# Delta-rule scan of a vision tower: the read-out products stored in four blocks of four k values

## The chip, the cores and the metric

The kernel runs on one core of one Trainium2 chip, as one launch. The metric is device time in microseconds (us): the median of 3 runs. Engines are named as in the profile: PE is TensorE (PEld its weight loads), DVE is VectorE, ACT is ScalarE, POOL is GpSimd, SP is SyncE.

## The reference, cut to what matters

The program is a tower of four pairs of layers (attention and feed-forward of four kinds each) over 32 images of 64 tokens with 256 features. The change is in the attention of the second pair, a gated delta rule: per image and head (32 x 16 = 512 states) a 16 x 16 matrix S is carried through the 64 tokens.

```
def step(S, inp):
    qt, kt, vt, at, bt = inp
    Sd = at[..., None, None] * S
    u = vt - jnp.einsum('bhk,bhkv->bhv', kt, Sd)
    Sn = Sd + bt[..., None, None] * kt[..., None] * u[:, :, None, :]
    o = jnp.einsum('bhk,bhkv->bhv', qt, Sn)
    return (Sn, o)
```

`o`, the read-out, is the sum over k of q[k] * S[k, v]. It is not needed by the next step; it is normed, projected and added to the stream after the scan.

## The kernel before

The 512 states lie on 128 partitions in 4 groups (`CG = 4`), so that a partition holds 4 x 16 x 16 = 1024 fp32 numbers of state, ordered g, v, k. Two copies of the state, `S[0]` and `S[1]`, stand in PSUM (`banks`, two banks each) and take turns. Groups 0 and 1 are half 0, groups 2 and 3 are half 1. Each engine has its instructions in an order written out by hand, with semaphores between them. One turn t of the 64 does this:

- DVE, `read_queries(t - 3)` (line 1820): state times q, 1024 elements, from PSUM into `products` in SBUF. It waits until the buffer is free (`o_summed_pair`).
- DVE, `read_keys(t)` (line 1811): state times k for each half, 512 elements, into `prod`. It waits for PE's `state0` and `state1` of turn t - 2.
- DVE, the reduce of line 1845: u of turn t out of `prod`.
- POOL: a correction for the next turn (line 1906), then the outer product of k and u (line 1911), 1024 elements.
- ACT, `fade` (line 1607): four copies of a state group from one S into the other, times the gate. It also places v (line 1599) and copies finished read-outs out of PSUM (line 1614).
- PE, `add_outer` (line 1464): for each half the outer product is added into the state in PSUM by a matmul of 512 columns against the identity. Then `sum_pair` (line 1473), one half of a read-out of two turns: 8 matmuls against the identity, one for each of 8 values of k, which add up the products over k in PSUM. Each reads 128 columns (2 turns x 64 pairs g, v). In 18 of the turns two or three matmuls of `sum_squares` follow (line 1482).

An fp32 matmul stands as two MATMUL records in the trace, each with its weight load. So a turn has 4 records of line 1464 and 16 of line 1473.

`products` reuses the memory of q, the tile `chain_q` in the rows. Its two ring places hold two turns (s) each. Before, an element's place is r, s, n, k with n = (g, v), so that the 128 columns that a matmul of one k reads stand 16 fp32 apart, 64 bytes.

Other instructions of the same layer read or write a 4-byte element at a distance, and their rows are used below. The last index of the operand's own layout gives the distance:

```
1755  dve.tensor_reduce(n2[:, g, :], o[:, g, :, :].rearrange("p d t -> p t d"), AX.X, ALU.add)   # 64 apart: 256 bytes
1789  dve.tensor_reduce(n2[:, g, 1:], dots.rearrange("p d t -> p t d"), AX.X, ALU.add)           # 63 apart: 252 bytes
1852  dve.tensor_reduce(n2[:, :, a:b], last_squares[n].rearrange("p g d t -> p g t d"), ...)     # 10 apart, then 2 apart: 40 and 8 bytes
1614  act.copy(o[:, :, :, 2 * n:2 * n + 2], ...)          # written in runs of 2 elements, 8 bytes
2244  act.copy(sel ...)                                   # written in runs of 4 elements, 16 bytes
1596  act.copy(qt[:, :, g, :].rearrange("p t d -> p d t"), q[:, g, :, :])   # written 64 apart: 256 bytes
```

Of the kernel before, what the change touches and what calls it, by code (L numbers as in the profile page):

```python
# [13 lines left out]
ALU = mybir.AluOpType  # L14
# [17 lines left out]
HD = D // HEADS  # L32
# [16 lines left out]
CG = 4  # L49
# [24 lines left out]
def bcast(ap, axis, n):  # L74

    ap = ap.unsqueeze(axis)
    shape = [int(s) for s in ap.shape]
    shape[axis] = n
    return ap.to_broadcast(shape)
# [1053 lines left out]
def vit_rest(nc, io, banks, H, ident, ident_bf, minus_half, const, const_in, scores_all, top, which, gate, xn_rows,  # L1133
# [4 lines left out]
    with ExitStack() as ctx:  # L1138
# [44 lines left out]
        with ExitStack() as work:  # L1183
# [3 lines left out]
            with ExitStack() as buffers:  # L1187
                experts = expert_layer(nc, buffers, work_sem, io, banks, ident, const, const_in, scores_all, top, which, gate,
                                       xn_rows, token_rows, lambda sp: [load(sp) for load in loads])
            delta = delta_layer(nc, work_sem, io, banks, H, ident, minus_half, token_rows, gate, chains, rates, front,  # L1190
                                delta_chain_buffers(nc, work), experts["all_sent"],
                                [sem(f"stored_o{g}") for g in range(CG)], first_load(0), first_load(1),
# [55 lines left out]
LASTS = ((CUTS[-1], TOK - TAIL), (TOK - TAIL, TOK))  # L1248
LAST = TOK - CUTS[-1]
ROW = HD + 2  # L1250
SUM_PARTS = ((0, 3), (3, 6), (6, 9), (9, 12), (12, 14), (14, HD))


# [27 lines left out]
def delta_layer(nc, sem, io, banks, H, ident, minus_half, token_rows, gate, chains, rates, front, chain, all_sent,  # L1281
# [15 lines left out]
    q, k, v, o = (chain[n] for n in "qkvo")  # L1297
    ka, kb, qt = (chain[n] for n in ("ka", "kb", "q_by_time"))
# [7 lines left out]
    flat = made_all[:, :, :].rearrange(states)  # L1306
    n_prod = 2 * CG * HD * ROW
    prod_ring = flat[:, 0:n_prod].rearrange("p (r g v x) -> p r g v x", r=2, g=CG, v=HD)
# [7 lines left out]
    dots = rows_flat[:, n_zero:n_zero + HD * (TOK - 1)].rearrange("p (d t) -> p d t", d=HD)  # L1316
    u_ring = rows_flat[:, n_zero:n_zero + 2 * CG * HD].rearrange("p (r g v) -> p r g v", r=2, g=CG)
    u = [u_ring[:, i, :, :] for i in range(2)]
    products = q[:, :, :, :].rearrange("p g d t -> p (g d t)").rearrange("p (r s n k) -> p r s n k", r=2, s=2, k=HD)
    link = rate[:, :, 0, :]  # L1320

    def state(b):
        return banks[:, b:b + 2, :].rearrange("p b (g v k) -> p (b g) v k", v=HD, k=HD)

    S = [state(0), state(2)]
# [5 lines left out]
    def o_n2(n):  # L1331
        return banks[:, 6, CG * CUTS[n]:CG * CUTS[n + 1]].rearrange("p (g t) -> p g t", g=CG)

    def chunk_squares(n):
        return squares[:, :, 0:CG * (CUTS[n + 1] - CUTS[n])]
# [82 lines left out]
    def tensor(pe):  # L1418
# [48 lines left out]
        def sum_pair(n, half):  # L1467
            if half == 0:
                pe.wait_ge(sem("q_made"), 2 * n + 2)
                if n > 1:  # L1470
                    pe.wait_ge(sem("o_made"), n - 1)
            for k in range(HD // 2 * half, HD // 2 * (half + 1)):
                ins = pe.matmul(o_sum[n % 2].rearrange("p (s n) -> p s n", s=2), ident[:, :],  # L1473
                                products[:, n % 2, :, :, k], start=(k == 0), stop=(k == HD - 1))
            if half:
                ins.then_inc(sem("o_summed_pair"), 1)

        def sum_squares(n, part):
            if part == 0:
                pe.wait_ge(sem("o_squared"), n + 1)  # L1480
            for d in range(*SUM_PARTS[part]):
                ins = pe.matmul(o_n2(n), ident[:, :], chunk_squares(n)[:, d, :]
                                .rearrange("p (g t) -> p g t", g=CG), start=(d == 0), stop=(d == HD - 1))
            if part == len(SUM_PARTS) - 1:
                ins.then_inc(sem("o_summed"), 1)
# [54 lines left out]
        for t in range(TOK):  # L1540
            for h in range(2):
                add_outer(t, h)
            if t >= 3:
                sum_pair((t - 3) // 2, (t - 3) % 2)
            for n in range(IN_STEPS):
                if 0 <= t - CUTS[n + 1] - 5 < len(SUM_PARTS):
                    sum_squares(n, t - CUTS[n + 1] - 5)
        sum_pair((TOK - TAIL) // 2 - 1, 1)

    def scalar(act):  # L1550
# [66 lines left out]
        def mean_out(n):  # L1617
            act.wait_ge(sem("o_summed"), n + 1)
            act.activation(n2[:, :, CUTS[n]:CUTS[n + 1]], o_n2(n), ACT.Identity, scale=1.0 / HD, bias=small[:, 0:1]
                           ).then_inc(sem("on_mean"), 1)  # L1620
# [6 lines left out]
        def square_out(n):  # L1627
            act.wait_ge(sem("o_made"), CUTS[n + 1] // 2)
            if n:
                act.wait_ge(sem("o_summed"), n)  # L1630
            act.square(chunk_squares(n).rearrange("p d (g t) -> p g d t", g=CG),
                       o[:, :, :, CUTS[n]:CUTS[n + 1]]).then_inc(sem("o_squared"), 1)
# [69 lines left out]
        for t in range(TOK):  # L1702
# [8 lines left out]
            for n in range(IN_STEPS):  # L1711
                if t == CUTS[n + 1] + 4:
                    square_out(n)
                if t == CUTS[n + 1] + 5 + len(SUM_PARTS):
                    mean_out(n)
# [11 lines left out]
    def vector(dve):  # L1727
# [86 lines left out]
        def read_queries(j):  # L1814
            n = j // 2
            for h in range(2):
                dve.wait_ge(sem(f"faded{h}"), j + 1)
            if n >= 2:
                dve.wait_ge(sem("o_summed_pair"), n - 1)
            dve.tensor_tensor(products[:, n % 2, j % 2, :, :].rearrange("p (g v) k -> p g v k", g=CG),  # L1820
                              S[j % 2], bcast(qt[:, j, :, :], 2, HD), ALU.mult
                              ).then_inc(sem("q_made"), 1)

        def read_last(j):
# [7 lines left out]
        for t in range(TOK):  # L1832
            if t == 3:
                dve.wait_ge(sem("q_turned"), CG)
            if t >= 3:
                read_queries(t - 3)
            read_keys(t)
            for h in range(2):
                dve.wait_ge(sem(f"prod_made{h}"), t + 1)
            dve.wait_ge(sem("values_placed"), t + 1)  # L1840
            if t:
                dve.wait_ge(sem("corrected"), t)
            if t >= 2:
                dve.wait_ge(sem("outer_made"), t - 1)
            dve.tensor_reduce(u[t % 2], prod[t % 2], AX.X, ALU.add).then_inc(sem("u_made"), 1)  # L1845
        read_queries(TOK - 3)
        dve.wait_ge(sem("u_made"), TOK)
        read_last(TOK - 2)
# [1125 lines left out]
```

## Time and profile before

| what | value |
|---|---|
| median of 3 runs | 1425.77 us (1425.03 to 1426.86) |
| the profiled execution: its time, its span | 1428.93 us, 1427.0 us |
| PE, DVE, ACT, POOL busy | 1269.4, 803.3, 512.3, 421.9 us |
| mean granted clock of TensorE | 0.952 |
| the scan | from 661 to 1010 us of the span |

The span is first to last instruction of the profiled execution; its own time is 1.9 us more, and 3.2 us over the median of the runs. A group of the trace is a source line with its engine, operation and tile; "idle before" is the time in which the engine stood still just ahead of it, with what ended the wait. Ends of matmuls are modelled, so that the distance of two starts is the safer measure on PE.

### The profile page before, as it was taken

What the parts mean: (1) busy time and instruction counts of PE and PEld (TensorE: products, weight loads), DVE (VectorE), ACT (ScalarE), POOL (GpSimd) and SP (SyncE); (2) the same over time, 40 slices, a digit from 0 to 9 for tenths busy, and PEclk for the clock granted to TensorE, in tenths of its full rate; (3) what the DMA queues carried; (4) which work ended last, traced back from release to release, by engine and by line L of the source; (5) the groups of instructions that cost most, each with busy time, mean ns of one, the idle gap of its engine ahead of it and who ended that gap; (6) DMA issues with size and microseconds to landing.
All of it is one profiled execution on the core that took longest, in us unless ns stands there. A gap on an engine that the chain in (4) does not pass through costs nothing. (4 is left out here: it accounts for less than half of the span.)

```text
span 1427.0 us, 25711 instructions
## 1 busy us (share of the span) xinstructions
PE 1269.4 (89%) x9667; PEld 1020.9 (72%) x9667; DVE 803.3 (56%) x1721; ACT 512.3 (36%) x1256; POOL 421.9 (30%) x573
## 2 busy tenths in 40 slices
PE   6999994898999999873999999999589999979975
PEld 4666674898999999630777877778467777766753
DVE  3666667111212211788777677676457777742587
ACT  2545451121121111543433333333124444435456
POOL 0111111232233332533444344343112212101465
PEclk9999997899999999995999999999899999999985
DMA  4111101898888883790000000000200004006721
GB/s 133 42 46 46 34 13 68 340 366 317 318 334 318 318 325 131 199 270 15 1 0 1 0 1 1 0 1 0 77 13 10 11 11 182 1 2 250 222 73 60
DMA packets 82714, 162.29 MB, mean 114 GB/s; under 512 B 42976, under 2 KB 61536, under 8 KB 76576
## 3 DMA queue, kind: packets, MB, share of 16 engines
q1 hardware_dynamic: 63776, 114.44, 23.5%
q0 software_dynamic: 10224, 44.05, 7.9%
q10 hardware_dynamic: 8592, 2.16, 0.7%
q8 instruction: 78, 1.28, 0.4%
q14 instruction: 44, 0.36, 0.1%
HBM read 134.28 MB, written 26.35 MB: 113 GB/s over the span
## 5 line engine op out<-in xcount | busy, mean ns | idle before, releaser
L1473 PEld LDWEIGHTS banks<-chain_q,ident 128*128 128x128 f32 x992 | 202.8, 204 | 39.3 <-issue 28.7
L1473 PE MATMUL banks<-chain_q,ident 128*128 128x128 f32 x992 | 226.2, 394 | 0.0
L936 PE MATMUL banks<-rowsT,w_up 128*128 128x128 f32 x1716 | 201.2, 278 | 0.2 <-DMA w_up<-in_up_w 0.2
L936 PEld LDWEIGHTS banks<-rowsT,w_up 128*128 128x128 f32 x1716 | 198.0, 195 | 0.5 <-DMA w_up<-in_up_w 0.4
L1464 PE MATMUL banks<-xT_d,ident 128*128 128x512 f32 x256 | 126.9, 618 | 31.4 <-POOL xT_d L1911 28.7
L1607 ACT ACTIVATE banks<-banks,rate 128x256 f32<-128x256 f32 x252 | 99.6, 446 | 136.8 <-DVE made L1811 132.7
L1911 POOL TENSOR_TENSOR xT_d<-kb,ys 128x1024 f32<-128x1024 f32 x64 | 123.3, 1927 | 3.7 <-DVE ys L1845 3.7
L1811 DVE TENSOR_TENSOR made<-banks,ka 128x512 f32<-128x512 f32 x128 | 86.0, 688 | 44.1 <-PE banks L1464 40.4
L950 PE MATMUL banks<-w_down,hT 128*128 128x256 f32 x468 | 107.5, 379 | 0.6 <-DVE res L1115 0.6
L1105 DVE TENSOR_TENSOR hT<-banks,silu 64x128 f32<-64x128 f32 x39 | 11.0, 283 | 168.0 <-ACT silu L993 168.0
L1820 DVE TENSOR_TENSOR chain_q<-banks,q_by_time 128x1024 f32<-128x1024 f32 x62 | 75.6, 1219 | 42.1 <-PE banks L1473 42.1
L1464 PEld LDWEIGHTS banks<-xT_d,ident 128*128 128x128 f32 x256 | 49.1, 200 | 70.0 <-issue 30.4
L950 PEld LDWEIGHTS banks<-w_down,hT 128*128 128x128 f32 x468 | 85.9, 190 | 11.0 <-issue 1.0
L1845 DVE TENSOR_REDUCE ys<-made 128x64 f32<-128x1152 f32 x64 | 86.6, 1353 | 5.7
L878 POOL DMA_DIRECT2D w_down<-in_down_w x39 | 22.2, 568 | 189.9 <-PE banks L950 181.7
L1906 POOL TENSOR_TENSOR made<-ys,rate 128x64 f32<-128x64 f32 x63 | 19.7, 313 | 198.0 <-DVE ys L1845 198.0
L2067 POOL TENSOR_TENSOR agg_b<-agg_b,minus_half 128x1 f32<-128x1 f32 x48 | 28.3, 590 | 158.8 <-DVE agg_b L2293 157.6
L983 ACT COPY rowsT<-banks 128x256 f32<-128x256 f32 x39 | 14.5, 373 | 147.0 <-PE banks L114 147.0
L1115 DVE COPY res<-banks 128x256 f32<-128x256 f32 x39 | 16.6, 425 | 75.2 <-PE banks L950 75.2
L468 PE MATMUL banks<-w_tok,patches 128*128 128x256 f32 x192 | 51.7, 408 | 7.1 <-DMA patches<-in_patches 7.1
L108 PE MATMUL banks<-ident 128*128 128x128 f32 x328 | 42.7, 286 | 12.1 <-PEq L92 12.1
L108 PEld LDWEIGHTS banks<-ident 128*128 128x128 f32 x328 | 40.9, 201 | 13.4 <-issue 13.0
(328 smaller groups left out, 2312.0 us busy)
## 6 DMA issues: line engine op xcount, KB each, us to landing
w_up<-in_up_w SPq DMA_DIRECT2D x39, 1408.0 KB, 6.1
w_down<-in_down_w POOLq DMA_DIRECT2D x39, 768.0 KB, 5.0
inter<-res_x SPq DMA_DIRECT2D x16, 512.0 KB, 4.0
back<-inter SPq DMA_DIRECT2D x15, 512.0 KB, 3.9
patches<-in_patches SPq DMA_DIRECT2D x16, 384.0 KB, 3.3
f<-in_f SPq DMA_DIRECT2D x6, 1024.0 KB, 11.8
ys<-token_rows SPq DMA_DIRECT2D x16, 256.0 KB, 2.9
xn_rows<-xn_all SPq DMA_DIRECT2D x16, 128.0 KB, 1.7
```

Of the source, the lines that this page charges most:

```text
L108: pe.matmul(out, ident, ident, start=True, stop=True, skip_group_check=True)
L468: ins = pe.matmul(X, patches[t % SLOTS_IN][:, c, :], w_tok[:, c, :], start=(c == 0), stop=(c == PC - 1), skip_group_check=True)
L936: ins = pe.matmul(out[:, m * P:(m + 1) * P], w[:, c, m * P:(m + 1) * P], x[:, c, :], start=(c == 0), stop=(c == 1))
L950: ins = pe.matmul(Y, hT[j % 2][:, c, :], w_down[j % DEEP][:, c, :], start=(c == 0), stop=(c == FULL))
L1464: pe.matmul(S[t % 2][:, halves[h], :, :], ident[:, :], outer[t % 2][:, halves[h], :, :], start=False, stop=True, skip_group_check=True).th ...
L1473: ins = pe.matmul(o_sum[n % 2].rearrange("p (s n) -> p s n", s=2), ident[:, :], products[:, n % 2, :, :, k], start=(k == 0), stop=(k == HD ...
L1607: ins = act.activation(S[t % 2][:, g, :, :].rearrange("p v k -> p (v k)"), S[(t + 1) % 2][:, g, :, :].rearrange("p v k -> p (v k)"), ACT.Copy,
L1811: dve.tensor_tensor(prod[t % 2][:, halves[h], :, 0:HD], S[t % 2][:, halves[h], :, :], bcast(ka[:, t, halves[h], :], 2, HD), ALU.mult).then ...
L1820: dve.tensor_tensor(products[:, n % 2, j % 2, :, :].rearrange("p (g v) k -> p g v k", g=CG), S[j % 2], bcast(qt[:, j, :, :], 2, HD), ALU.m ...
L1845: dve.tensor_reduce(u[t % 2], prod[t % 2], AX.X, ALU.add).then_inc(sem("u_made"), 1)
L1911: pool.tensor_tensor(outer[t % 2], bcast(kb[:, t, :, :], 2, HD), bcast(u[t % 2], 3, HD), ALU.mult).then_inc(sem("outer_made"), 1)
L2067: pool.tensor_tensor(agg[n][:, 1:2], agg[n][:, 1:2], minus_half[:, 0:1], ALU.pow).then_inc(sem(f"ln{n}_rstd"), 1)
```

## The change

The products are stored as r, s, b, n, k with b = 4 blocks of 4 values of k. DVE makes the same 1024 products with one instruction, and writes them in runs of 4 (16 bytes) instead of in one run; what it reads is as before. PE reads the same 128 columns for each k, in the same order, now 4 fp32 (16 bytes) apart. No instruction is added, removed or moved on any engine, and no semaphore changes.

```
+RUN = 4
...
-    products = q[:, :, :, :].rearrange("p g d t -> p (g d t)").rearrange("p (r s n k) -> p r s n k", r=2, s=2, k=HD)
+    products = q[:, :, :, :].rearrange("p g d t -> p (g d t)").rearrange("p (r s b n k) -> p r s b n k", r=2, s=2, b=HD // RUN, k=RUN)
...
+    def in_runs(x):
+        return x.rearrange("p b (g v) k -> p g v b k", v=HD)
+
+    def cut_runs(x):
+        return x.rearrange("p g v (b k) -> p g v b k", k=RUN)
...
                 ins = pe.matmul(o_sum[n % 2].rearrange("p (s n) -> p s n", s=2), ident[:, :],
-                                products[:, n % 2, :, :, k], start=(k == 0), stop=(k == HD - 1))
+                                products[:, n % 2, :, k // RUN, :, k % RUN], start=(k == 0), stop=(k == HD - 1))
...
-            dve.tensor_tensor(products[:, n % 2, j % 2, :, :].rearrange("p (g v) k -> p g v k", g=CG),
-                              S[j % 2], bcast(qt[:, j, :, :], 2, HD), ALU.mult
+            dve.tensor_tensor(in_runs(products[:, n % 2, j % 2]),
+                              cut_runs(S[j % 2]), cut_runs(bcast(qt[:, j, :, :], 2, HD)), ALU.mult
```

## Rows read from the trace of the kernel before

**Rows 1.** Page, costliest groups: busy us, mean ns of one, idle before, releaser

```profile
L1473 PE MATMUL banks<-chain_q,ident 128*128 128x128 f32 x992 | 226.2, 394 | 0.0
L1464 PE MATMUL banks<-xT_d,ident 128*128 128x512 f32 x256 | 126.9, 618 | 31.4 <-POOL xT_d L1911 28.7
L1811 DVE TENSOR_TENSOR made<-banks,ka 128x512 f32<-128x512 f32 x128 | 86.0, 688 | 44.1 <-PE banks L1464 40.4
L1820 DVE TENSOR_TENSOR chain_q<-banks,q_by_time 128x1024 f32<-128x1024 f32 x62 | 75.6, 1219 | 42.1 <-PE banks L1473 42.1
```

**Rows 2.** Stretches of the scan: length, busy us of each engine, granted clock, DMA

```profile
core 0: us, PE busy (x) PEld busy (x) DVE busy (x) ACT busy (x) POOL busy (x), PEclk, DMA share, GB/s
680.00:760.00 80.00, 80.00 (x310) 62.68 (x309) 60.14 (x64) 31.00 (x86) 34.36 (x31) 1.00 0.00 1
860.00:1000.00 140.00, 140.00 (x575) 110.97 (x574) 98.15 (x103) 52.60 (x142) 54.34 (x49) 1.00 0.00 1
```

**Rows 3.** Timeline, first turns with read-out sums: start us, us, engine, line

```profile
677.98 1.35 DVE L1845 TENSOR_REDUCE ys<-made 128x64 f32<-128x1152 f32 x1
...
679.25 1.22 DVE L1820 TENSOR_TENSOR chain_q<-banks,q_by_time 128x1024 f32<-128x1024 f32 x1
...
679.80 3.65 PE L1473 MATMUL banks<-chain_q,ident 128*128 128x128 f32 x16
...
680.38 1.28 DVE L1811 TENSOR_TENSOR made<-banks,ka 128x512 f32<-128x512 f32 x2
...
681.75 1.35 DVE L1845 TENSOR_REDUCE ys<-made 128x64 f32<-128x1152 f32 x1
683.02 1.21 DVE L1820 TENSOR_TENSOR chain_q<-banks,q_by_time 128x1024 f32<-128x1024 f32 x1
...
685.01 3.65 PE L1473 MATMUL banks<-chain_q,ident 128*128 128x128 f32 x16
...
688.48 1.90 PE L1464 MATMUL banks<-xT_d,ident 128*128 128x512 f32 x4
...
690.21 3.65 PE L1473 MATMUL banks<-chain_q,ident 128*128 128x128 f32 x16
```

**Rows 4.** Timeline, the last turns of the scan

```profile
989.21 0.80 PE L1482 MATMUL banks<-w_delta,ident 128*128 128x64 f32 x6
...
989.84 1.94 PE L1464 MATMUL banks<-xT_d,ident 128*128 128x512 f32 x4
...
992.59 1.35 DVE L1845 TENSOR_REDUCE ys<-made 128x64 f32<-128x1152 f32 x1
...
994.03 1.93 POOL L1911 TENSOR_TENSOR xT_d<-kb,ys 128x1024 f32<-128x1024 f32 x1 [3.69 <-DVE ys L1845]
...
995.09 0.57 PE L1482 MATMUL banks<-w_delta,ident 128*128 128x64 f32 x4
...
995.49 1.94 PE L1464 MATMUL banks<-xT_d,ident 128*128 128x512 f32 x4
...
1002.92 7.14 PE L1473 MATMUL banks<-chain_q,ident 128*128 128x128 f32 x32
...
1010.09 0.27 ACT L1614 COPY chain_o<-banks 128x128 f32<-128x128 f32 x1 [8.43 <-PE banks L1473]
```

**Rows 5.** Timeline of PE: 128 columns read in one run

```profile
1044.40 1.95 PE L2174 MATMUL banks<-x2T,arena 128*128 128x128 f32 x16
1046.28 0.99 PE L261 MATMUL banks<-arena,x2T 128*64 128x128 f32 x14
```

**Rows 6.** Groups by shape, DVE: 256, 252, 40 and 8 bytes apart, then contiguous

```profile
L1755 DVE TENSOR_REDUCE n<-chain_o 128x64 f32<-128x1024 f32 x4 | 7.7, 1923 | 7.7 <-ACT chain_o L1592 7.7
L1789 DVE TENSOR_REDUCE n<-ys 128x63 f32<-128x1008 f32 x4 | 7.7, 1926 | 0.0
L1852 DVE TENSOR_REDUCE n<-made 128x40 f32<-128x640 f32 x1 | 1.3, 1279 | 5.9 <-ACT made L1636 5.9
L1852 DVE TENSOR_REDUCE n<-made 128x8 f32<-128x128 f32 x1 | 0.3, 276 | 0.0
L679 DVE TENSOR_REDUCE neg<-banks 128x16 f32<-128x1024 f32 x16 | 19.5, 1216 | 1.2 <-PE banks L231 1.2
L2341 DVE TENSOR_REDUCE best<-logits 128x8 f32<-128x128 f32 x16 | 4.6, 286 | 0.5
```

**Rows 7.** Groups, ACT: writes in runs of 2 and 4, 256 bytes apart, contiguous

```profile
L1614 ACT COPY chain_o<-banks 128x128 f32<-128x128 f32 x31 | 8.5, 273 | 66.1 <-PE banks L1473 66.1
L1588 ACT ACTIVATE rate_made<-banks 128x128 f32<-128x128 f32 x4 | 1.1, 273 | 3.3 <-DMA rates<-rate_made 1.9 <-ACT made L1571 1.4
L2244 ACT COPY sel<-banks 128x512 f32<-128x512 f32 x32 | 17.2, 590 | 4.3 <-PE banks L2132 4.0
L636 ACT COPY PT<-banks 128x512 f32<-128x512 f32 x16 | 9.4, 586 | 4.2 <-PE banks L240 4.1
L1596 ACT COPY q_by_time<-chain_q 128x1024 f32<-128x1024 f32 x4 | 8.3, 2076 | 12.0 <-DMA chain_q<-chains_q 11.0 <-ACT made L1571 1.0
L1592 ACT ACTIVATE chain_o<-chain_k 128x1024 f32<-128x1024 f32 x4 | 4.3, 1066 | 4.8 <-DMA chain_k<-chains_k 4.8
```

## The prediction

> **What bounds the scan now.** I read the page's groups first, then the scan by stretches, then its timeline. In the groups [rows 1] the reader is to see who stands still. PE has 31.4 us of idle time before line 1464, of which 28.7 are a single wait ahead of the first turn; before line 1473 it has none. DVE waits 42.1 us for PE's line 1473 (a product buffer is not yet free) and 40.4 us for line 1464 (the state is not yet added). By stretches [rows 2] PE is busy for 80.00 of 80 us and 140.00 of 140, at a granted clock of 1.00 (2.4 GHz), while DVE is busy for 60.14 and 98.15. So PE sets the pace, and DVE has room.
>
> The timeline gives PE's turn by starts [rows 3]: 16 records of line 1473 from 685.01 to 688.48 are 3.47 us, or 217 ns each; 4 records of line 1464 from 688.48 to 690.21 are 1.73 us. A turn is 5.20 us. In 18 turns square sums lie between: 6 records in 12 of them, 989.21 to 989.84, 0.63 us, and 4 records in 6, 995.09 to 995.49, 0.40 us [rows 4]. From turn 3, whose sums start at 679.80, to turn 63, at 1002.92, that makes 60 x 5.20 + 12 x 0.63 + 6 x 0.40 = 322.0 us; the trace has 323.1. So the engine does nothing else, and 3.47 of its 5.20 us are the reads that the change touches.
>
> DVE's own turn, where it does not wait, is the distance of two line 1820 starts, 679.25 to 683.02: 3.77 us [rows 3]. Its room is 5.20 - 3.77 = 1.43 us a turn.
>
> **The change, part by part.** No instruction is added, removed or moved, so there are two costs: PE's read at 16 bytes between columns, 992 records, and DVE's write in runs of 16 bytes, 62 products.
>
> *PE's read.* 128 columns at 64 bytes take 217 ns, 1.70 ns a column. 128 columns in one run take 117 ns (16 records from 1044.40 to 1046.28 [rows 5]). So the distance costs 100 ns a record. The trace has no matmul that reads at 16 bytes; the two rows are its bounds, 217 and 117 ns.
>
> Which of them? DVE's rows [rows 6] tell how the price goes with the distance. A contiguous reduce of 1024 elements takes 1216 ns and one of 128 takes 286, so 1.04 ns an element and about 150 ns of start. At 256 bytes: (1923 - 150) / 1024 = 1.73 ns. At 252 bytes: 1776 / 1008 = 1.76. At 40 bytes: 1129 / 640 = 1.76. At 8 bytes, 276 ns for 128 elements: no price at all. So it is a step and no slope: the same 1.7 ns from 40 bytes to 256, on DVE as on PE, and nothing at 8. What fits all of them is a memory that hands out one stretch of bytes every 1.7 ns, so that an element alone in its stretch pays it. The stretch holds two elements 8 bytes apart, and the elements at 40 bytes never share one. If it were 64 bytes, elements at 40 bytes would need 5 stretches for 8 elements, which at 1.7 ns is 1.06 ns an element, all but free; they pay in full. That leaves 16 or 32 bytes. With 16, each column of the new layout is alone and pays 217 ns as before; with 32 two share one and it takes 117. As distances, 16 lies no nearer to the paying row (40) than to the free one (8), so distance does not decide it. I take the smaller stretch, three to one, because it already carries every row: it gives 16 bytes in 1.7 ns, four fp32 numbers, and no row of the scan needs more than one in 0.9 ns. So 992 x (217 - 217) = 0.
>
> The Trainium skill bears on just this choice (SBUF — State Buffer, in the note on cachelines under "Door 1: The DMA port swizzle"). It gives SBUF lines of 16 bytes and asks for at least two hits on a line for full bandwidth; by that rule the columns at 16 bytes pay as those at 64 do, and the sum is 0. The rows at 8, 40 and 256 bytes agree with it, and none here shows 16.
>
> *DVE's write.* Its price is bounded by ACT's writes [rows 7]. 128 elements in runs of two take 273 ns, as 128 contiguous ones do (273); 512 in runs of four, 16 bytes as here, take 590 against 586. Written singly at 256 bytes, 1024 take 2076 against 1066. So between nothing and the single price, which on DVE's 1024 would be (1.76 - 1.04) x 1024 = 0.74 us. I take nothing, by the row with the same runs. Even 0.74 lies within DVE's room of 1.43 us a turn; without that cover (if PE became faster) it would be paid in full. What DVE reads is as before.
>
> *Sum.* The profiled execution stays at 1428.93 us (span 1427.0). That run lies 3.2 us over the median of the runs, so the median forecast is the one shown: **1425.8 us**, within 0.2% (2.9 us, about what a measurement of this kernel can tell from no change). PE's turn stays 5.20 us, and the same waits of DVE stay where they are.
>
> **Rivals.**
>
> *A: the read at 16 bytes is free.* PE's turn falls to 16 x 0.117 + 1.73 = 3.60 us, or 4.23 and 4.00 with square sums, and DVE with 3.77 becomes the bound in the others. From turn 4 (reduce at 677.98 [rows 3]) to turn 63 (992.59 [rows 4]) are 59 turns: 314.6 us now; 41 x 3.77 + 12 x 4.23 + 6 x 4.00 = 229 then, 85 less. If ACT's fades, which stand between DVE and PE in each turn, stretch a turn to 4.2 us, it is 248, 67 less. After the reduce of turn 63 the last read-out copy starts 17.5 us later now (1010.09). Then POOL's last product, which starts 1.44 and ends 3.37 us after that reduce [rows 4], no longer meets a queue on PE: two halves of line 1464 take 2 us, 32 records of 117 ns 3.7, so some 9.5, and 8 us less. Together 75 to 93 less: 1333 to 1351, say 1342. For it: the free row at 8 bytes, and that a stretch of 32 bytes is not excluded. Against it: the smaller stretch carries all rows.
>
> The same note of the Trainium skill says next that one can stride for free up to 4 fp32, which taken at its word is this change, and rival A with its 1342. It does not go together with two hits a line, and no row here shows it.
>
> *B: free on PE, but DVE pays for its new runs*, or PE gains only half. With 0.74 us more DVE's turn is 4.51: 59 x (5.33 - 4.51) = 48, with the 8 of the end 56 less: 1370. Half the gain on PE (167 ns) makes its turn 4.40 and gives 60 x 0.80 + 32 x 0.05 = 50 less: 1376. Against the first speaks the run row of ACT, against the second that no price between 1.04 and 1.7 ns stands in any row.
>
> *C, slower: DVE pays for each run.* A product now has 256 runs. DVE's 1.43 us of room is used up at 5.6 ns a run; from there on the excess counts. At 7 ns a product takes 1.79 us more and DVE's turn is 5.56: 0.36 us in each of the 41 turns without square sums, 15 us: 1441. Against it: ACT's 128 runs in line 2244 cost 4 ns altogether.
>
> That the change doesn't do what it says is no rival: the program reads PE's columns at 4 elements and writes DVE's runs of 4.
>
> **How the numbers follow.** The read pays as before, with DVE's write hidden: 0.75; of that 0.02 fall by chance out of 0.2% on either side. A 0.16, B 0.05, C 0.04. So faster 0.16 + 0.05 + 0.01 = 0.22, slower 0.04 + 0.01 = 0.05, the same 0.73. The likeliest case alone has 1423 to 1429. That holds less than 8 in 10, so the range reaches over B into A: 1340 to 1429 leaves out the lower half of A, C, and a little else, some 0.14.
>
> **What the profile of the changed kernel would show.** Right: starts of line 1480 (1473 before) still 217 ns apart, PE busy throughout 680 to 1000 us, DVE's product (1827) at 1.22 us, and DVE's two waits for PE still near 40 us each. Wrong by A: starts near 117 ns, PE with idle time that ends with ACT's fades or with DVE, DVE's waits for line 1480 gone, the scan ended near 925 us. Wrong by B or C: the product at 1.9 us or more, PE waiting for DVE. What would make the forecast wrong is above all one number, the size of the stretch that PE's read gets at once.

## The result, and the profile after

The changed kernel takes 1443.64 us (median of 4 runs, 1440.79 to 1447.06) against 1425.4 us of the kernel before (1424.49 to 1426.86): a ratio of 1.0128 with a 95% interval of 1.0104 to 1.0153. It is 18 us slower, where no change was forecast. (Here and below, a ratio with its interval comes from all executions and need not be the quotient of the two medians.) The profiled execution took 1442.81 us, its span is 1440.9 us.

In the changed kernel the lines of the scan stand 7 further down: 1464 is 1471, 1473 is 1480, 1811 is 1818, 1820 is 1827, 1845 is 1852. Its groups, as [rows 1]:

```profile
L1480 PE MATMUL banks<-chain_q,ident 128*128 128x128 f32 x992 | 234.7, 404 | 0.0
L1471 PE MATMUL banks<-xT_d,ident 128*128 128x512 f32 x256 | 124.1, 607 | 33.4 <-POOL xT_d L1918 29.0 <-ACT banks L1614 4.2
L1818 DVE TENSOR_TENSOR made<-banks,ka 128x512 f32<-128x512 f32 x128 | 85.9, 688 | 47.0 <-PE banks L1471 43.3
L1827 DVE TENSOR_TENSOR chain_q<-banks,q_by_time 128x1024 f32<-128x1024 f32 x62 | 75.6, 1220 | 46.0 <-PE banks L1480 46.0
```

DVE's product costs what it did (1220 ns after 1219). PE's read-out sums are 8.5 us dearer (234.7 after 226.2), one record 404 ns after 394 (two records overlap in time, so the distance of starts below is the safer measure), and DVE waits a little longer for PE at both places. The line's first and last record, then the timeline of the scan, as [rows 3, 4]: one turn early, and the end.

```profile
L1480 PE MATMUL banks<-chain_q,ident x992: 386/405/408, 676.1 to 1014.4; 128*128 128x128 f32 x199
```

```profile
686.75 3.79 PE L1480 MATMUL banks<-chain_q,ident 128*128 128x128 f32 x16
...
690.36 1.90 PE L1471 MATMUL banks<-xT_d,ident 128*128 128x512 f32 x4
...
692.09 3.79 PE L1480 MATMUL banks<-chain_q,ident 128*128 128x128 f32 x16
...
1014.85 0.27 ACT L1621 COPY chain_o<-banks 128x128 f32<-128x128 f32 x1 [8.71 <-PE banks L1480]
```

Sixteen records fill 686.75 to 690.36: 226 ns each, where it was 217. The adds still take 1.73 us. So a turn is 5.34 us instead of 5.20. From the first sums (at 676.1 us) to the last copy the scan takes 338.8 us after 330.3: 8.5 us more, which is 992 records at 8.6 ns.

The rest lies behind the scan. From the last copy to the end of the span it was 416.9 us and is 426.1: 9.1 us more, in layers that the diff does not touch. (Ahead of the scan this execution was 3.7 us quicker; -3.7 + 8.5 + 9.1 is the 13.9 us between the spans.) Where the 9 us arise is seen in stretches of 10 us near the end of the middle layers; the third number from the right is the granted clock. The kernel before:

```profile
1250.00:1260.00 10.00, 7.48 (x89) 5.56 (x87) 6.19 (x16) 3.72 (x9) 1.10 (x2) 1.00 0.00 0
1260.00:1270.00 10.00, 7.83 (x117) 6.37 (x115) 3.07 (x9) 3.72 (x10) 0.55 (x1) 1.00 0.01 2
1270.00:1280.00 10.00, 6.60 (x66) 5.02 (x67) 5.38 (x11) 3.43 (x6) 0.00 (x0) 1.00 0.01 2
```

The changed kernel, where the same instructions stand some 4 us later:

```profile
1255.00:1265.00 10.00, 7.48 (x82) 5.30 (x80) 5.49 (x13) 3.80 (x9) 0.65 (x2) 0.87 0.01 2
1265.00:1275.00 10.00, 8.95 (x78) 7.82 (x77) 1.71 (x4) 3.28 (x8) 0.00 (x0) 0.62 0.00 0
1275.00:1285.00 10.00, 7.49 (x62) 5.09 (x61) 4.93 (x11) 3.08 (x7) 0.55 (x1) 0.73 0.01 2
```

The clock goes from 2.4 to 1.2 GHz in the second kernel and not in the first. What PE did just ahead of it is the same in both. Before, and the first matmuls of the layers that follow:

```profile
1256.75 0.41 PE L114 MATMUL banks<-ident,H 128*128 128x128 f32 x2 [1.12 <-DVE H L2298]
1257.62 0.71 PE L2120 MATMUL banks<-x3T,arena 128*128 128x128 f32 x4 [0.46 <-ACT x3T L2234]
1259.05 1.14 PE L2132 MATMUL banks<-spread,H 64*128 64x256 f32 x8 [0.71 <-DVE probs_b L2324]
...
1289.56 1.97 PE L2519 MATMUL banks<-sel,f 128*64 128x128 f32 x32 [2.39 <-PEq L92]
```

After:

```profile
1260.97 0.41 PE L114 MATMUL banks<-ident,H 128*128 128x128 f32 x2 [1.12 <-DVE H L2305]
1261.84 0.71 PE L2127 MATMUL banks<-x3T,arena 128*128 128x128 f32 x4 [0.46 <-ACT x3T L2241]
1263.27 2.08 PE L2139 MATMUL banks<-spread,H 64*128 64x256 f32 x8 [0.71 <-DVE probs_b L2331]
...
1301.99 1.97 PE L2526 MATMUL banks<-sel,f 128*64 128x128 f32 x32 [2.39 <-PEq L92]
```

The same three waits of 1.12, 0.46 and 0.71 us stand in both; behind them the eight records of the selection take 1.14 us in one and 2.08 in the other. From these waits to the next layers the changed kernel's lateness grows from 4.2 us (1260.97 against 1256.75) to 12.4 (1301.99 against 1289.56). So the code and the waits ahead of the fall are the same in both executions and do not decide by themselves. That this place is reached later is one difference, and that was put to the test.

### The profile page after: what moved, and what is told of

Same layout as the page of the kernel before. It is cut to its first block and busy times, and to the rows that moved or that the text cites. A ratio compares the mean times of both kernels' runs of the same rounds, so it can differ in the third digit from the quotient of the medians.

```text
span 1440.9 us, 25711 instructions
## 1 busy us (share of the span) xinstructions
PE 1280.6 (89%) x9667; PEld 1027.7 (71%) x9667; DVE 804.4 (56%) x1721; ACT 511.2 (35%) x1256; POOL 421.5 (29%) x573
## 5 line engine op out<-in xcount | busy, mean ns | idle before, releaser
L1480 PE MATMUL banks<-chain_q,ident 128*128 128x128 f32 x992 | 234.7, 404 | 0.0
L1827 DVE TENSOR_TENSOR chain_q<-banks,q_by_time 128x1024 f32<-128x1024 f32 x62 | 75.6, 1220 | 46.0 <-PE banks L1480 46.0
```

Of the source, the lines that this page charges most:

```text
L1827: dve.tensor_tensor(in_runs(products[:, n % 2, j % 2]), cut_runs(S[j % 2]), cut_runs(bcast(qt[:, j, :, :], 2, HD)), ALU.mult).then_inc(sem ...
```

## The experiments

Two questions were open: is the 8.6 ns a record the price of 16 bytes, or of the jump between two halves of 64 columns, which the new layout also brings; and is the part behind the scan caused by the delay alone?

**One distance instead of two halves.** The two turns s are put inside the block, so that all 128 columns stand 16 bytes apart:

```
-products = ... .rearrange("p (r s b n k) -> p r s b n k", ...)
+products = ... .rearrange("p (r b s n k) -> p r b s n k", ...)
...
-products[:, n % 2, :, k // RUN, :, k % RUN]
+products[:, n % 2, k // RUN, :, :, k % RUN]
...
-in_runs(products[:, n % 2, j % 2])
+in_runs(products[:, n % 2, :, j % 2])
```

> Blocks of four k as in the change, but with the two turns next to each other inside a block (order r, b, s, n, k), so that the 128 columns of a matmul stand at one distance of 16 bytes and no longer in two halves of 64. Theory (the 8.6 ns more of each record in the change come from the jump between the two halves; 16 bytes cost just what 64 cost): starts 217 ns apart, PE's turn 5.20 us, the scan 323 us from turn 3 to turn 63 as before, 1425 us if what comes after the scan is as before. Rival (16 bytes between columns cost more than 64, whatever the pattern): starts 226 ns apart, 331 us, 1434 to 1444 us. Second rival (16 bytes in one sequence are free): starts 117 ns, about 1342 us.

Measured: 1442.7 us (1434.94 to 1444.73) against 1430.01 (1422.91 to 1438.82, 14 executions) of the kernel before on the same chip, ratio 1.0086 (1.0042 to 1.013). The line's record has the same median as in the change, 405 ns:

```profile
L1480 PE MATMUL banks<-chain_q,ident x992: 386/405/408, 676.6 to 1014.9; 128*128 128x128 f32 x199
```

My theory of the jump fell: the price belongs to the 16 bytes. This profiled execution (1439.44 us) did not meet the fall of the clock that the change's did:

```profile
1204.80:1294.80 90.00, 77.13 (x851) 61.61 (x849) 55.30 (x142) 35.18 (x82) 11.79 (x21) 1.00 0.05 18
```

Even so it took 422.3 us from its last copy (1015.35) to the end, 5.4 more than the kernel before, in smaller pieces whose cause stays open. So the 9.1 us behind the scan are those of one execution and no fixed price.

**Eight bytes.** `RUN = 2` in the changed kernel, nothing else.

> The change with RUN = 2: 8 bytes between PE's columns, DVE writes runs of two. Theory (memory gives 16 bytes every 1.7 ns, and a column that is alone in them pays): two columns share a stretch, starts 117 to 126 ns apart, PE's turn 3.6 to 3.75 us, DVE with 3.77 us a turn becomes the bound, its waits for the read-out sums vanish, 1333 to 1355 us. Rival (any distance between PE's columns costs the same, and only a contiguous read is fast): starts 217 to 226 ns, 1425 to 1444 us. A third outcome (DVE pays for runs of two): product near 1.9 us, about 1370 us.

Measured: 1334.59 us (1333.07 to 1340.17), ratio 0.9341 (0.9292 to 0.9389). Groups, then two turns of the timeline:

```profile
L1480 PE MATMUL banks<-chain_q,ident 128*128 128x128 f32 x992 | 122.4, 275 | 0.0
...
L1827 DVE TENSOR_TENSOR chain_q<-banks,q_by_time 128x1024 f32<-128x1024 f32 x62 | 75.3, 1215 | 0.0
```

```profile
681.64 1.21 DVE L1827 TENSOR_TENSOR chain_q<-banks,q_by_time 128x1024 f32<-128x1024 f32 x1
...
685.41 1.22 DVE L1827 TENSOR_TENSOR chain_q<-banks,q_by_time 128x1024 f32<-128x1024 f32 x1
...
913.66 0.27 ACT L1621 COPY chain_o<-banks 128x128 f32<-128x128 f32 x1 [5.09 <-PE banks L1480]
```

A record takes 275 ns, as it does where it reads in single runs (`RUN = 1`, next); DVE's wait ahead of its product, 42.1 us before, is gone, and its turn is the 3.77 us that [rows 3] gave where it did not wait. The bound has moved from PE to DVE, but for the turns with square sums: near the end their sums start at 893.48 and 897.68, 4.20 us apart. (PE still counts as busy for 100.00 us of 760 to 860, and DVE for 96.27; the starts and the waits tell which of them sets the pace.) From the first sums (678.4) to the last copy the scan takes 235 us instead of 330.3: 95 us less.

**Four bytes.** `RUN = 1`: PE reads in runs, DVE writes singly.

> The change with RUN = 1: PE reads each half of its columns in one run, DVE writes every product singly at 256 bytes. Theory: PE's starts 117 ns apart, or 126 if the jump between the two halves costs 8.6 ns; DVE's product pays 0.7 ns more an element, 1.95 us, DVE's turn 4.5 us and the bound: about 1370 us. Rival (PE's price does not depend on the distance but on something else in the read): starts still 217 to 226 ns, 1425 to 1444 us.

Measured: 1370.1 us (1368.38 to 1377.13), ratio 0.9592 (0.9539 to 0.9644). PE's record is 275 ns, DVE's product 1983:

```profile
L1480 PE MATMUL banks<-chain_q,ident x992: 272/275/276, 679.9 to 950.4; 128*128 128x128 f32 x199
...
701.48 1.99 DVE L1827 TENSOR_TENSOR chain_q<-banks,q_by_time 128x1024 f32<-128x1024 f32 x1
703.29 1.29 DVE L1818 TENSOR_TENSOR made<-banks,ka 128x512 f32<-128x512 f32 x2
704.67 1.35 DVE L1852 TENSOR_REDUCE ys<-made 128x64 f32<-128x1152 f32 x1
705.94 1.98 DVE L1827 TENSOR_TENSOR chain_q<-banks,q_by_time 128x1024 f32<-128x1024 f32 x1
```

DVE's turn is 4.46 us: the price has moved from PE's read to DVE's write, 0.76 us a product. Runs of two and of four cost DVE nothing (1215 and 1220 ns).

**All distances, on a tile that nobody writes.** Each of the 16 matmuls reads `kb` at a distance of its own, on a line of its own; the sums, and with them the layer's output, are not the read-out any more.

```
-products[:, n % 2, :, :, k]
+still[:, 0:128:1]    +still[:, 0:255:2]    +still[:, 0:382:3]    +still[:, 0:509:4]    ...
```

> A measurement on the kernel before: the 16 matmuls of a read-out read 128 columns each from a tile that nobody writes during the scan (kb), each at a distance of its own: 4, 8, 12, 16, 20, 24, 32, 48 bytes, then 64, 80, 96, 128, 16 and 64 shifted by 4 bytes, 28 and 40. The layer's output is left wrong by it; DVE makes its products as before. Theory (memory gives 16 bytes every 1.7 ns, a column alone in them pays): 4 and 8 bytes 117 ns; 12 bytes between (four columns in three stretches), near 163; 16 and all others 217 to 226. For the 9 ns more at 16 than at 64: if they come from the distance itself, 16 bytes show 226 and 64 show 217 here as well; if from DVE writing the tile that PE reads, both show 217. Rival (32 bytes in a stretch): 16 bytes already falls by the change's own trace, so this rival is out.

Measured, in a turn with the distances 64, 80, 96, 128, 16 and 64 (these two shifted by 4), 28 and 40 bytes, and the turn after it with 4, 8, 12, 16, 20, 24, 32 and 48:

```profile
761.75 0.59 PE L1492 MATMUL banks<-kb,ident 128*128 128x128 f32 x2
762.17 0.71 PE L1494 MATMUL banks<-kb,ident 128*128 128x128 f32 x2
762.70 0.83 PE L1496 MATMUL banks<-kb,ident 128*128 128x128 f32 x2
763.33 0.64 PE L1498 MATMUL banks<-kb,ident 128*128 128x128 f32 x2
763.79 0.63 PE L1500 MATMUL banks<-kb,ident 128*128 128x128 f32 x2
764.25 0.61 PE L1502 MATMUL banks<-kb,ident 128*128 128x128 f32 x2
764.68 0.64 PE L1504 MATMUL banks<-kb,ident 128*128 128x128 f32 x2
765.15 0.64 PE L1506 MATMUL banks<-kb,ident 128*128 128x128 f32 x2
765.60 1.90 PE L1464 MATMUL banks<-xT_d,ident 128*128 128x512 f32 x4
...
767.34 0.38 PE L1476 MATMUL banks<-kb,ident 128*128 128x128 f32 x2
767.56 0.39 PE L1478 MATMUL banks<-kb,ident 128*128 128x128 f32 x2
767.79 0.50 PE L1480 MATMUL banks<-kb,ident 128*128 128x128 f32 x2
768.12 0.62 PE L1482 MATMUL banks<-kb,ident 128*128 128x128 f32 x2
768.57 0.64 PE L1484 MATMUL banks<-kb,ident 128*128 128x128 f32 x2
769.03 0.64 PE L1486 MATMUL banks<-kb,ident 128*128 128x128 f32 x2
769.48 0.65 PE L1488 MATMUL banks<-kb,ident 128*128 128x128 f32 x2
769.95 0.63 PE L1490 MATMUL banks<-kb,ident 128*128 128x128 f32 x2
770.40 1.90 PE L1464 MATMUL banks<-xT_d,ident 128*128 128x512 f32 x4
```

Half the distance of two starts is a record: 110 ns at 4 bytes, 115 at 8, 165 at 12, 225 to 230 at 16 and 225 to 235 at 20, 24, 28, 32, 40 and 48; then 210 to 215 at 64, 265 at 80, 315 at 96 and 230 at 128. I had expected 217 to 226 for all from 16 bytes on; 80 and 96 lie far off. The 12 bytes come out where the stretch of 16 bytes puts them (163). And 16 bytes are some 15 ns dearer than 64 here too (225 after 210, shifted 230 after 215), on a tile at rest: that DVE writes the tile that PE reads is not the cause.

**A delay alone.** In the kernel before, PE runs 37 idle matmuls, meant to take about 8.5 us, ahead of the last sums:

```
+        keep_warm(pe, banks[:, 4, 0:P], ident[:, :], 37)
         sum_pair((TOK - TAIL) // 2 - 1, 1)
```

> The kernel before, with 37 idle matmuls (74 records, about 8.5 us) on PE ahead of the very last half of the read-out sums, so that all that follows the scan comes some 8.5 us later and nothing else changes. Theory (the part of the change's loss that lies after the scan, about 9 us, comes from layers that start at another time and find TensorE at a lower granted clock): 1434 plus up to 9, so 1438 to 1444 us, with a stretch of granted clock under 0.9 near the end of the middle layers. Rival (a delay costs just itself): 1434 us, with the granted clock at 1.00 in that stretch as before.

Measured: 1441.68 us against 1430.01, ratio 1.0058 (1.0024 to 1.0091). The idle matmuls took 8.3 us:

```profile
1004.72 8.44 PE L108 MATMUL banks<-ident 128*128 128x128 f32 x74
1012.99 3.65 PE L1473 MATMUL banks<-chain_q,ident 128*128 128x128 f32 x16
```

The ten executions fall into two heaps: 1431.9 to 1435.0 (three) and 1441.0 to 1444.9 (seven). The profiled one is of the second, and its clock was low near the end of the middle layers:

```profile
1210.00:1300.00 90.00, 78.95 (x803) 63.82 (x803) 50.19 (x131) 31.09 (x73) 11.34 (x20) 0.87 0.01 1
```

From its last copy (1016.67) to the end it took 426.3 us, as the changed kernel did (426.1). So the fall needs nothing of the new layout. That lateness brings it about is not shown. The two heaps go with the mean granted clock of an execution (0.957 to 0.958 and 0.943 to 0.949), and the kernel before has such heaps on this chip as well: eight executions with 0.952 to 0.957 took 1422.9 to 1430.3 us, six with 0.945 to 0.948 took 1430.8 to 1438.8. None of the six has a trace, so where they lost the clock is not known. Seven of ten against six of 14 is no clear difference, and the ratio over all executions, 0.58% of 1430 or 8.3 us (by its interval 3.4 to 13.0), is just what the idle matmuls took.

**The idle places filled.** In the two turns ahead of the last one of the middle layers PE gets 2 to 5 idle matmuls in each of four waits, in the kernel before and in the changed one:

```
+(4, warm(4, {end - 2: 4, end - 1: 5})), (4, warm(6, {end: 11})), (4, turn_x3), (5, select_first), (4, warm(4, {end - 2: 2, end - 1: 2})), ...
+(4, warm(4, {end - 2: 3, end - 1: 3})), (5, warm(6, {end: 3})), (5, select_last), ... (4, warm(4, {end - 2: 3, end - 1: 3})), (3, attend)
```

> The kernel before with idle matmuls (4 to 5, 2, 3 and 3 of them) in PE's waits in the last turns but one of the middle layers, where the clock fell in the change's trace. Theory (the fall of the clock there is a matter of when the layer begins, and PE's idle stretches allow it): the clock stays 1.00 there in every execution, 1423 to 1428 us, and the spread of the executions becomes smaller than the 16 us of the kernel before on the same chip. Rival (the fall has another cause): spread and median as for the kernel before.

> The change with the same idle matmuls. Theory: what is left of its loss is the scan's own, 992 records at 8.6 ns, so 8.5 us over the run e6_before_warm, near 1433 us. Rival (the change slows the later layers in another way): still 15 us or more over it.

Measured side by side, 12 executions each: 1427.05 us (1424.46 to 1430.88) for the kernel before, 1435.72 (1431.47 to 1439.96) for the change; against the plain kernel before (1428.67, 23 executions from 1424.2 to 1438.3) the ratios are 0.9976 (0.9953 to 0.9998) and 1.0038 (1.0015 to 1.0061). The two filled kernels lie 8.7 us apart, the scan's own 8.5; by the spread of the 24 executions I estimate that this is good to about 2 us. All 24 have a mean granted clock of 0.951 to 0.957, where ten of the 23 of the plain kernel have 0.943 to 0.949: filling these places takes the heap with the lower clock away. Four of the 12 of the filled kernel before still lie above the 1428 us that I expected at most. In both profiles the granted clock of 1200 to 1290 us is 1.00, here that of the change; a short stay at 1.2 GHz is left in it after 1290 us:

```profile
1200.00:1290.00 90.00, 83.43 (x938) 68.32 (x935) 56.02 (x145) 35.87 (x85) 13.08 (x22) 1.00 0.10 40
1240.00:1300.00 60.00, 52.96 (x589) 43.59 (x587) 28.64 (x72) 20.51 (x47) 6.00 (x17) 0.97 0.03 8
```

**The best of both.** `RUN = 2` with these idle matmuls.

> Blocks of two k values with the same idle matmuls. The scan as in the run e2_run2 (235 us from the first sums to the last); if the clock fell there as well, some 5 us less than that run's 1334.6: 1325 to 1332 us. If the idle matmuls cost more than they keep, 1335 to 1340.

Measured: 1328.66 us (1326.5 to 1331.19), ratio 0.9285 (0.9242 to 0.9328), the fastest version found.

## Why the prediction was wrong

- **What bounds the scan** was right: PE's turn, with 3.47 us in the touched reads. Halving the read (`RUN = 2`) brought what rival A was worked out for, 1335 us where A had 1333 to 1351, with DVE's turn at 3.77 us. The scan alone took 95 us less, a little more than A's 75 to 93.
- **The choice of the stretch** was right: 16 bytes and not 32. 12, 16 and 8 bytes on a tile at rest show it. The two-hits rule of the Trainium skill (SBUF — State Buffer, the note on cachelines under "Door 1: The DMA port swizzle") agrees with that; the sentence after it, by which 4 fp32 are free, does not agree with the 225 ns measured at 16 bytes, and the measurement decides.
- **The step that failed first** is the term 992 x (217 - 217) = 0. I took the single price for the same at every distance, because DVE's rows had 1.73 to 1.76 ns from 40 to 256 bytes [rows 6]. PE's own row at 64 bytes was the only one at a distance that I had for PE, and 64 turned out to be the cheapest of the single distances. The record at 16 bytes takes 226 ns, and PE has no room: 992 x 8.6 ns = 8.5 us, all on the path. That alone makes 1434, outside the range. 8.6 ns a record are 0.07 ns a column; DVE's rows already differed by 0.03 ns an element between 256 bytes and 252 or 40, and I had rounded over it. Whether the two have one cause no run here tells.
- **DVE's write** was right: nothing for runs of four. Rival C's sign came true and its mechanism did not; that its 1441 lies near the 1444 measured is luck. No rival had PE's read dearer than before.
- **The step that was missing** is what stands behind the scan. The sum ended with the scan and let the rest of the program stay as it was. About half of the 18 us (9.1 in the profiled execution) arose there, most of it in the stretch where TensorE's clock fell to 1.2 GHz, in layers that only come later. With the idle places filled the two kernels lie 8.7 us apart, so beyond the scan's 8.5 the new layout costs no more than the 2 us that this comparison can tell. Which executions meet the fall stays open: the waits ahead of it are the same in both kernels, and that a later start brings it about is not shown, as the delay of 8.3 us cost 8.3 us on the whole. So the size of the 18 us has chance in it: all four executions of the kernel before took 1424.5 to 1426.9 us, as its later ones with the higher clock did (1422.9 to 1430.3), while the profiled one of the change had the fall.
- **The range** ended at 1429 because its upper side held only the measurement's spread, and that spread was taken too small: 2.9 us, where later executions of the same kernel went from 1422.9 to 1438.8. And where the engine that bounds the scan is busy for 80.00 of 80 us, any error in the price of its work shows in the time; the upper side had no room for one.

## What to carry to other kernels

Where TensorE bounds a stage and reads fp32 at a distance, try pairs: here, with two neighbouring elements side by side, the read ran nearly like a contiguous one (115 ns after 110), and VectorE wrote pairs at no price. Reading in single runs (`RUN = 1`) only moved the price to VectorE's write. A price that one row gives for one distance should be carried to another distance with an error: 4% from 64 to 16 bytes here, half as much again to 96, and on a full engine that error counts in full. And if the clock falls in some executions and not in others in layers that a change does not touch, compare many executions, or both kernels with the short idle places there filled, before putting a loss down to the change.

## What was not expected of the hardware

PE's price is not one step: on a tile at rest a record of 128 columns takes 265 ns at 80 bytes and 315 at 96, against 210 to 215 at 64 and 230 at 128. Why 80 and 96 bytes cost most, and 64 the least of the single distances, no run here tells.
